# Differential attention with experts behind it: the exponentials turned to queries on the partitions, the difference of the two softmaxes formed before the values are weighed

## The reference, cut to what matters

```python
s1 = einsum('bhtd,bhsd->bhts', q1, k1) * scale + mask      # causal
s2 = einsum('bhtd,bhsd->bhts', q2, k2) * scale + mask
diff = softmax(s1) - lam * softmax(s2)
out = einsum('bhts,bhsd->bhtd', diff, v)
mean, var = mean and variance of out over (t, d), for each head
out = (out - mean) * rsqrt(var + EPS) * gn_w + gn_b
y = out.reshape(B, T, 512) * 0.8 @ Wo
x2 = layernorm(x + y)
# then for every token: a shared SwiGLU, and one of 8 experts
# (router, top 1, gate); result = layernorm(x2 + both)
```

## Time and profile before

| | us |
|---|---|
| median of 3 runs | 824.52 |
| lowest, highest | 824.46, 827.38 |
| the profiled execution itself | 826.78 |
| its span, first to last instruction | 825.1 |

### The profile page before, as it was taken

The page is one execution under the profiler, slowest core; times in us unless marked ns, Lnnn a source line. Parts: engine busy times, 40 slices in busy tenths (PEclk is TensorE's granted clock), DMA queues, the critical chain, the costliest instruction groups (busy, mean ns, idle before and its releaser), DMA issues.

```text
span 825.1 us, 11250 instructions
## 1 busy us (share of the span) xinstructions
PE 740.3 (90%) x3890; PEld 407.1 (49%) x3890; DVE 471.5 (57%) x1040; ACT 316.6 (38%) x584; POOL 308.1 (37%) x263
## 2 busy tenths in 40 slices
PE   7588899999889999997899997899999798999993
PEld 3233334334334444543444444444326557999993
DVE  2756886763657876446678754576525342334332
ACT  2415544444555334355553331655663011111110
POOL 4057711120984131139721210321420034666653
...
GB/s 132 146 340 168 18 187 83 19 22 40 1 26 183 87 35 27 21 46 24 48 159 45 58 0 84 160 2 0 36 49 1 26 193 213 267 267 243 234 123 1
DMA packets 55831, 78.73 MB, mean 95 GB/s; under 512 B 11543, under 2 KB 43037, under 8 KB 53920
## 3 DMA queue, kind: packets, MB, share of 16 engines
...
## 4 chain that ended last, share of the span: by engine, by line
PE 69%; DVE 13%; POOL 6%; issue 5%; DMA 3%; ACT 2%; SPq 1%; POOLq 0%; DVEq 0%; ACTq 0%
PE pv_ps L1017 16%; PE wide_ps L1097 10%; PE s_ps L856 7%; PE wide_ps L1003 7%; DVE mneg L1435 6%; PE wide_ps L844 5%; PE wide_ps L987 3%; PE s_ps L888 3%; PE s_ps L857 3%; PE wide_ps L959 3%; PE misc L1108 2%; PE pv_ps L1108 2%; PE misc L934 2%; POOL w_exp L1348 2%; PE wide_ps L992 2%
## 5 line engine op out<-in xcount | busy, mean ns | idle before, releaser
L1435 DVE TENSOR_REDUCE mneg<-s_ps 128x1 f32<-128x384 f32 (+3 forms) x352 | 215.5, 638 | 96.3 <-PE s_ps L857 92.5
L1216 ACT ACTIVATE w_exp<-wide_ps 128x512 f32<-128x512 f32 x320 | 178.9, 601 | 102.7 <-PE wide_ps L1003 101.2
L1017 PE MATMUL pv_ps<-w_exp,work 128*64 128x512 f32 x640 | 176.7, 633 | 3.0 <-ACT work L1234 1.9
L1348 POOL TENSOR_SCALAR_AFFINE_SELECT w_exp<-w_exp 128x1024 f32<-128x1024 f32 x64 | 70.7, 1108 | 278.8 <-ACT w_exp L1216 278.8
L856 PE MATMUL s_ps<-w_exp 96*128 96x256 bf16 (+3 forms) x512 | 129.9, 313 | 17.5 <-DVE mneg L1435 9.4
L1003 PE MATMUL wide_ps<-w_exp 98*128 98x512 bf16 x320 | 122.4, 397 | 15.4 <-ACT w_exp L1216 14.0
L1003 PEld LDWEIGHTS wide_ps<-w_exp 98*128 98x128 bf16 x320 | 31.0, 102 | 154.0 <-ACT w_exp L1216 83.3
L857 PE MATMUL s_ps<-mask,identb 128*128 128x128 bf16 (+2 forms) x352 | 89.1, 253 | 0.0
L1097 PE MATMUL wide_ps<-tables,w_exp 128*128 128x128 f32 x736 | 85.9, 275 | 0.0
L1097 PEld LDWEIGHTS wide_ps<-tables,w_exp 128*128 128x128 f32 x736 | 84.1, 192 | 0.1
L856 PEld LDWEIGHTS s_ps<-w_exp 96*128 96x128 bf16 x512 | 45.1, 100 | 62.9 <-DVE mneg L1435 37.2
...
...
## 6 DMA issues: line engine op xcount, KB each, us to landing
...
```

The lines of the kernel that those rows point to most:

```text
L1017: last = nc.tensor.matmul(pv_ps[s * 64:(s + 1) * 64, :], vo[:, kt, g, :], probs[:, n % NP, s, :], start=(kt == 0), stop=(kt == qt))
L1216: nc.scalar.activation(probs[:, n % NP, s], st_bank(v), ACT.Exp, scale=float(DH) ** -0.5).then_inc(st_done, 1)
L1348: nc.gpsimd.affine_select(out=e, in_=e, compare_op=ALU.is_ge, fill=0.0, base=0, pattern=[[0, 8], [1, P]], channel_multiplier=-1).then_inc( ...
L1435: nc.vector.tensor_reduce(out=mneg[:, qt, rows[0]:rows[-1] + 1], in_=s_ps[:, (v - 1) % 2, 0:len(rows) * w].rearrange("p (r k) -> p r k", r ...
```

## The change

The steps (qt, g, kt) are replaced by 44 groups a batch, (qt, first head r, heads, g), numbered K over all batches: 4 groups of 4 heads for qt 0, 8 of 2 heads for qt 1, 16 of one head for qt 2 and 16 of one head for qt 3. For each group and each of the two softmaxes s:

- `score_bank` fills a bank with queries on the partitions, as before, but in a ring of four banks, which the projections of `prep` share. There are no other scores.
- DVE takes the maxima (`maximum`) and ACT the exponentials (`exponents`) straight from that bank, one instruction for each head, with the negated maximum as bias and the sum of the row as a second output. The factor of the scores now lies in the tables of the rotation.
- Two groups later DVE (`subtract`) takes reciprocals for two groups at once, the ratio of the sums times -lambda, and for each head e1 + ratio * e2, an operation with two inputs in SBUF. POOL (`make_diag`) makes for each head a diagonal matrix of 1/sum1.
- Four groups later PE (`turn_diff`) multiplies each 128x128 tile of the difference with that diagonal matrix in f32, which turns it and divides it; ACT (`take_diff`) copies the result to SBUF.
- For every four groups (a "quad", all g) PE weighs the values once (`weigh`), the four g in four strips of 32 columns of the array; ACT copies a query tile's sums (`take_out`).

The output then lies with channels on the partitions: DVE takes mean and variance with its batch-norm instructions (`stat`), PE averages over channels, POOL subtracts the mean (4 operations over 512 columns), and neither squares nor turns are needed. The detour of the maxima through memory, the column of ones and POOL's zeroing are gone. `prep` moves into the steps 0 to 7 of the batch before, POOL's 18 operations into steps 4 to 28. The `x2` of two batches share a buffer's two halves. In the tail the late steps of the last groups (`drain`) stand between the late gates of the shared SwiGLU.

The diff, cut to its core:

```diff
-NP = 4
+NPROB, NDIFF, NTURN = 4, 3, 5
...
+PER_BANK = [max(1, QT // (qt + 1)) for qt in range(QT)]
+GROUPS = [(qt, r, PER_BANK[qt], g) for qt in range(QT) for r in range(0, 4, PER_BANK[qt]) for g in range(KV)]
...
+LAG_DIFF, LAG_TURN, LAG_WEIGH, LAG_OUT = 2, 4, 8, 9
...
+put(0, ("v", 0, 0))
+for _k in range(8):
+    put(_k, ("prep", _k, 0))
+put(6, ("stat", 1, 1))
+put(8, ("mean", 0, 1))
+put(10, ("var", 0, 1))
+put(11, ("scale", 0, 1), ("scale", 1, 1))
+for _t in range(QT):
+    put(12 + 2 * _t, ("project", _t, 1))
+    put(13 + 2 * _t, ("x2", _t, 1))
+    put(15 + 2 * _t, ("retake", _t, 1))
+    put(16 + 2 * _t, ("logits", _t, 1))
+put(18, ("stat", 0, 0))
+put(20, ("bias", 0, 0))
+put(23, ("top", 0, 1))
+put(24, ("choose", 0, 1))
...
+RING = 4
+RING_USES = [("start", 0, k) for k in range(8)] + [("prep", 0, arg) for name, arg, _ in HEAD if name == "prep"]
+for _b in range(B):
+    for _k in range(NG):
+        RING_USES += [("bank", _b, 2 * _k), ("bank", _b, 2 * _k + 1)]
+        RING_USES += [("prep", _b, arg) for name, arg, _ in tasks_at(_b, _k) if name == "prep"]
...
-PREP_LATER = [1, 3, 3, 3, 4, 5, 5, 6, 6, 7, 7, 7, 9, 10, 10, 11, 13, 14]
+PREP_FIRST = [-4, -4, -3, -3, 5, 6, 8, 9, 11, 12, 14, 16, 17, 18, 20, 22, 24, 26]
+PREP_LATER = [4, 5, 7, 8, 10, 11, 13, 14, 16, 17, 18, 20, 21, 23, 24, 26, 27, 28]
...
+            def score_bank(b, k, s):
+                qt, r, heads, g = GROUPS[k]
+                v = bank_at(b, k, s)
+                pe.wait_ge(ring_done, v - RING)
                 w = (qt + 1) * P
-                keys = k_stack[:, b % 2]
-                o = s_ps[:, (v - 1) % 2, 0:len(rows) * w].rearrange("p (n k) -> p n k", k=w)
-                for n, hs in enumerate(rows):
-                    nc.tensor.matmul(o[:, n], q_stack[0:KROWS, qt, hs, :], keys[0:KROWS, hs // 4, 0:qt + 1, :], start=(n == 0), stop=False)
-                last = nc.tensor.matmul(o[:, :, w - P:w], identb[:], mask[:].unsqueeze(1).to_broadcast([P, len(rows), P]), start=False, stop=True)
-                last.then_inc(bank_full, 1)
+                o = ring(v)[:, 0:heads * w].rearrange("p (n k) -> p n k", k=w)
+                for n in range(heads):
+                    nc.tensor.matmul(o[:, n], q_stack[0:KROWS, qt, (2 * g + s) * 4 + r + n, :], k_stack[0:KROWS, b % 2, 2 * g + s, 0:qt + 1, :],
+                                     start=(n == 0), stop=False)
+                last = nc.tensor.matmul(o[:, :, w - P:w], identb[:], mask[:].unsqueeze(1).to_broadcast([P, heads, P]), start=False, stop=True)
...
+            def turn_diff(K):
+                b, k, qt, r, heads, g = group(K)
+                pe.wait_ge(diff_done, K + 1)
+                pe.wait_ge(diag_ready, K + 1)
+                if K >= 2:
+                    pe.wait_ge(diff_taken, K - 1)
+                w = (qt + 1) * P
+                for n in range(heads):
+                    for kt in range(qt + 1):
+                        at = n * w + kt * P
+                        last = nc.tensor.matmul(s_ps[:, K % 2, at:at + P], diffs[K % NDIFF][:, at:at + P], diag_unit(UNIT[K] + n),
+                                                start=True, stop=True)
+                last.then_inc(diff_turned, 1)
+            def weigh(J):
+                b, j = divmod(J, NQUAD)
+                qt, r, heads, _ = GROUPS[KV * j]
+                pe.wait_ge(diff_taken, KV * (J + 1))
+                if j == 0:
+                    pe.wait_ge(far_done, values_at[b])
+                if KV * j == FIRST_G[qt] and b * QT + qt > 0:
+                    pe.wait_ge(out_taken, b * QT + qt)
+                for kt in range(qt + 1):
+                    for g in range(KV):
+                        d = turned_d[(KV * J + g) % NTURN][:, 0:heads * (qt + 1) * P].rearrange("p (n k q) -> p n k q", n=heads, k=qt + 1)
+                        last = nc.tensor.matmul(pv_ps[g * DV:(g + 1) * DV, r * P:(r + heads) * P].rearrange("p (n q) -> p n q", n=heads),
+                                                vo[:, b % 2, kt, g, :], d[:, :, kt, :], start=(kt == 0), stop=(kt == qt))
+                last.then_inc(quad_done, 1)
+            def lagging(K):
...
-            def scores(b, n, s):
-                qt, g, kt = STEPS[n]
-                v = st_at(b, n, s)
-                if s == 0 and n == FIRST_ST[qt]:
-                    pe.wait_ge(max_loaded[qt], (b + 1) * 16)
-                pe.wait_ge(st_done, v - RING)
-                gs = 2 * g + s
-                nc.tensor.matmul(st_bank(v), k_stack[0:MROWS, b % 2, gs, kt, :],
-                                 q_stack[0:MROWS, qt, gs * 4:gs * 4 + 4, :], start=True, stop=True).then_inc(st_full, 1)
-            def weigh(b, n):
-                qt, g, kt = STEPS[n]
-                u = qt * KV + g
-                if kt == qt:
-                    pe.wait_ge(diag_done, b * NUNIT + DIAG.index(n) + 1)
-                else:
-                    pe.wait_ge(st_done, st_at(b, n, 1))
-                if kt == 0:
-                    if b * NUNIT + u > 0:
-                        pe.wait_ge(pv_done, b * NUNIT + u)
-                for s in range(2):
-                    last = nc.tensor.matmul(pv_ps[s * 64:(s + 1) * 64, :], vo[:, kt, g, :], probs[:, n % NP, s, :],
-                                            start=(kt == 0), stop=(kt == qt))
-                last.then_inc(pv_step, 1)
-            def body(b, prep_next, post):
...
+            def exponents(K):
+                b, k, qt, r, heads, g = group(K)
+                w = (qt + 1) * P
+                if K >= NPROB:
+                    act.wait_ge(diff_done, K - NPROB + 1)
+                for s in range(2):
+                    act.wait_ge(max_done, 2 * K + s + 1)
+                    v = bank_at(b, k, s)
+                    for n in range(heads):
+                        ins = nc.scalar.activation(probs[:, K % NPROB, s, n * w:(n + 1) * w], ring(v)[:, n * w:(n + 1) * w], ACT.Exp,
+                                                   bias=mneg[:, (2 * K + s) % 4, n:n + 1], scale=1.0,
+                                                   accum_out=total[:, K // 2 % 2, K % 2, s, n:n + 1])
+                    ins.then_inc(ring_done, 1)
+            def take_diff(K):
+                b, k, qt, r, heads, g = group(K)
+                act.wait_ge(diff_turned, K + 1)
+                if K >= NTURN:
+                    act.wait_ge(quad_done, (K - NTURN) // KV + 1)
+                w = heads * (qt + 1) * P
+                nc.scalar.copy(turned_d[K % NTURN][:, 0:w], s_ps[:, K % 2, 0:w]).then_inc(diff_taken, 1)
...
+                    pool.wait_ge(mean_ready, b + 1)
+                    for r in range(4):
+                        ins = nc.gpsimd.tensor_scalar(zT[:, r], oT[:, r], head_mean[:, r:r + 1], None, ALU.subtract)
+                    ins.then_inc(centred, 1)
...
+            def make_diag(K):
+                b, k, qt, r, heads, g = group(K)
+                pool.wait_ge(sums_turned, K // 2 + 1)
+                if UNIT[K + 1] > NUNIT:
+                    pool.wait_ge(diff_turned, unit_owner(UNIT[K + 1] - 1 - NUNIT) + 1)
+                for n in range(heads):
+                    ins = nc.gpsimd.tensor_scalar(diag_unit(UNIT[K] + n), ident[:], rl[:, K // 2 % 3, K % 2, 0, n:n + 1], None, ALU.mult)
+                ins.then_inc(diag_ready, 1)
...
+            def subtract(K):
+                b, k, qt, r, heads, g = group(K)
+                pair = K // 2 % 2
+                if K % 2 == 0:
+                    b2, k2 = group(K + 1)[:2]
+                    dve.wait_ge(ring_done, bank_at(b2, k2, 1))
+                    nc.vector.reciprocal(rl[:, K // 2 % 3, :, :, 0:heads], total[:, pair, :, :, 0:heads]).then_inc(sums_turned, 1)
+                    dve.wait_ge(sums_turned, K // 2 + 1)
+                    c.link(nc.vector.scalar_tensor_tensor(ratio[:, pair, :, 0:heads], total[:, pair, :, 0, 0:heads], neglam[:],
+                                                          rl[:, K // 2 % 3, :, 1, 0:heads], ALU.mult, ALU.mult))
+                if K >= NDIFF:
+                    dve.wait_ge(diff_turned, K - NDIFF + 1)
+                w = (qt + 1) * P
+                for n in range(heads):
+                    here = slice(n * w, (n + 1) * w)
+                    ins = nc.vector.scalar_tensor_tensor(diffs[K % NDIFF][:, here], probs[:, K % NPROB, 1, here], ratio[:, pair, K % 2, n:n + 1],
+                                                         probs[:, K % NPROB, 0, here], ALU.mult, ALU.add)
+                ins.then_inc(diff_done, 1)
...
-                    c.link(nc.vector.reciprocal(rl[:], t[:, :, :, DV]))
-                    nc.vector.tensor_tensor(o12[:], t[:, :, :, 0:DV], rl[:].unsqueeze(3).to_broadcast([P, 4, 2, DV]), ALU.mult).then_inc(near_done, 1)
-                    dve.wait_ge(near_done, v)
-                    c.link(nc.vector.scalar_tensor_tensor(att[:, qt, g * 4:g * 4 + 4, :], o12[:, :, 1], neglam[:], o12[:, :, 0],
-                                                          ALU.mult, ALU.add))
...
```

719 lines of the change are left out of this document (256 added, 463 removed).

## The result

The changed kernel takes 839.65 us at the median (835.77 to 843.71) beside 825.42 for the kernel before, a ratio of 1.0186 (95% interval 1.015 to 1.0221): slower by 1.9%, where 836 was forecast. The time is close, but most of the terms that it was added up from were not; their errors cancel, which is luck.

What follows compares the result with a forecast made beforehand. PE, busy 147.7 of 158.7 us in a middle batch, was taken as the bound. Middle batches -7, batch 0 -12, batch 3 +17, tail -3.5 sum to -5.5; 826.8 - 5.5 + 17 of coupling, less 2.3, gives 836 (812 to 862).

Steps and rivals of the forecast that it cites:

- PE is relieved, and no other engine takes its full place: Middle batch: PE falls from 147.7 to 125 us; the stages, paced by ACT or DVE, sum to 155 against 158.6.
- serial strips: Rival, in the weighing: the strips don't run together, PE +23 us a batch, 863 us in all; chance 0.12.
- the lower clock: Rival: PE, less busy in batches 0 and 3, gets a lower clock; a few us at most, within the forecast.
- The exponentials: ACT: 128 a batch at 0.44 to 0.78 us; ACT sets groups 0 to 11 at 47 us.
- the rival of 0.2 us per sum: Each row sum costs ACT 0.2 us, so ACT takes over: +7 us a batch, 864 us in all; chance 0.2.
- Locks: DVE's two-input operations wait for POOL's: 1.0 us for each of 11 long operations in qt 2, plus matrices.
- The matrices: POOL's diagonal matrices in qt 2 and 3: 0.33 us charged to DVE per group, for one matrix each.
- qt 3: Groups 28 to 43: 51 us in middle batches, 42 in batches 0 and 3, including 5 of locks.
- the 0.9 that I named as a sign: Differences of 512 columns on DVE would have a mean over 0.9 us, against 0.68 alone.
- Coupling: Engines near their limits in a ring two groups deep: 3% of 571 us, +17 us.
- The tail: After batch 3: fewer turns, but a chain of mean, centring on POOL, variance, scale; -3.5 us.
- rival of PE's gain coming through: Sums and locks cost nothing, so PE's saved time shows: 740 us, half of it, 788, expected; chance 0.26.

Runs made afterwards that it cites:

- e6: The changed kernel with PE turning every difference of qt 2 twice: 831.11 us, ratio 1.005 to the kernel before.
- f2: e8 and e6 together on the changed kernel, rotations still on POOL: 821.08 us, ratio 0.9923 to the kernel before.
- e5: The changed kernel with exponentials that store no row sums, a constant in their place: 828.88 us, ratio 1.0046 to the kernel before.
- e4: The changed kernel without POOL's 18 rotations and splits a batch: 795.92 us, ratio 0.9651 to the kernel before.
- e3: The changed kernel without POOL's diagonal matrices from the third group on: 840.31 us, ratio 1.0204 to the kernel before.
- e7: The changed kernel with the 18 rotations and splits a batch on DVE instead of POOL: 832.08 us, ratio 1.0081 to the kernel before.
- g1: The changed kernel with e8, e6 and e7's edits, and the last batch's projections, turns and logits spread over separate groups: 807.85 us, ratio 0.9786.
- e8: The changed kernel with the tail's last turnings and weighings before the late SwiGLU, and centring on DVE: 826.32 us, ratio 1.0002.

## Why the prediction was right, and where its steps failed

- **PE is relieved, and no other engine takes its full place.** Right. The strips run together: in the tail the 32 instructions of one weighing of 512 columns, four strips, start within 0.8 us (629.56 to 630.36), and the weighings occupy PE for 48 us in all, 12 a batch, where I took 11; serial strips would be 3.6 us each time. That rival is out. PE's busy time is 681, not 650, and the clock is the reason: of the 144 us at the lower level PE is busy in 106 (before, in 52 of 72). At half the speed, as in the projection's 1.9 and 3.8 us, that makes 27 us more of busy time, an estimate. I had put the lower clock at "a few us at most". Lifting part of it gave back 11 us in e6 and 6.5 in f2. This step failed.
- **ACT.** The exponentials were priced at 0.44, 0.55, 0.67 and 0.78 us; from start to start they are 0.34, 0.45, 0.56 and 0.68, about 0.1 less each. The mis-sized term is the base of 0.56, busy time divided by count, which counts the overlap of two rows only where they happen to follow one another. Back to back, the old exponentials start 0.48 us apart:

```profile
606.62 1.09 ACT L1216 ACTIVATE w_exp<-wide_ps 128x512 f32<-128x512 f32 x2 [0.73 <-PE wide_ps L1003]
```

The pointer's 0.11 agrees (the new one in e5, without sums, takes 0.585 against 0.477), and so does the sum's (0.095); the rival of 0.2 us per sum is out. By the forecast's own prices that rival's groups should have been 4.8 and 3.1 us for qt 0 and 1, not 5.0 and 3.3, and its time about 9 us less. Groups 0 to 11 took 47.7 us against 47, but with ACT busy in 37.9 of them, not 47: the right number came from the wrong engine, and that is luck. In e5 these groups give back 1 us for 6.1 us of sums.
- **Locks.** The long operations were right where I charged them: 10 us in qt 2, and DVE's busy time there falls by 10.6 us (batch 1) and 9.5 (batch 2) in e4. They cost 3 us more each in groups 0 to 11 and in qt 3, where I had charged none. The matrices were to cost 5 us in qt 2 and 5 in qt 3 and cost nothing that shows (e3). So 20 us a batch were charged and 14.7 measured (DVE's 44 us over three batches). The matrix itself takes 0.68 us where I took 0.33. The rule of the Trainium skill ("SBUF — State Buffer", "Who interferes with whom"), an exclusive lock between a two-input operation and POOL's, agrees with e4 and e7.
- **qt 3** was priced too dear. In batch 3, where no long operation of `prep` runs, its groups take 34.2 us instead of 42, in e3 without matrices 34.5: the 5 us of locks by matrices aren't there. DVE is busy 33 of these 34 us, so it is the bound, and its maxima start 0.60 us apart where I took 0.67. A difference of 512 columns takes 0.80 us on the mean, not the 0.9 that I named as a sign. The 7.8 us that qt 3 came out cheaper are more than the 5.7 us by which batch 3 came out below the forecast, and its 4.3 us in batch 0 are half of the 8.6 there.
- **Coupling.** 3% was added without a mechanism. Middle batches have 6.0 us over my sum (161.0 against 155), 3.9%, all of it in groups 12 to 27. g1 shows one mechanism, router tasks that hand over `misc` in one group, worth 3 us a batch; the lower clock is another, and the rest stays open. In batches 0 and 3 there was nothing of it over the sum.
- **The tail** was the worst term: -3.5 forecast, +16.4 measured, a part of which is work of batch 3 that stood ahead of the boundary before. I named the chain of mean, centring on POOL, variance and scale, and then gave it no time, nor did I look at the late pieces between the last turnings. Centring costs POOL 6.2 us. e8, with both put right, gives back 8.7 us.
- **Sum.** Batches 0 and 3 14 us too dear, tail 20 too cheap, 17 of coupling where the middle batches needed 12: the errors cancel to 1 us in the profiled execution. The 2.3 us that I took off for that execution did not come again, and the median lies 3.7 us over the forecast. The forecast's direction came from batch 3 and from the coupling, 17 us each; the measured one came from the tail (+16.4), batch 3 (+11.4) and the middle batches (+5), against -20.6 in batch 0. The rival of PE's gain coming through gets nearer when these places are repaired: g1, at 807.85, is over half of the way from 839.65 to its 788.
